# A 16-head attention inside a long kernel: batch 1's projections and splits moved in front of the loop

## The reference

```
Q, K, V = x @ Wq.T + bq, x @ Wk.T + bk, x @ Wv.T + bv      # split into 16 heads of 16
lam = 10 * exp(-5 * u_prev);  use_sparse = lam >= 1
dense  = softmax(Q K^T / 4 + lam * (mask ? 0 : -1)) V
sparse = softmax over 32 chosen keys per query (with their multiplicity) V
out = where(use_sparse, sparse, dense) @ Wo.T + bo
```

## Time and profile before

| | us |
|---|---|
| median of 3 runs (2247.75 to 2248.11) | 2247.83 |
| the profiled execution | 2237.77 |
| its span | 2235.9 |
| TensorE busy | 1931.1 (86%) |
| VectorE busy | 1138.5 (51%) |
| ScalarE busy | 933.5 (42%) |
| POOL busy | 441.0 (20%) |

### The profile page before, as it was taken

One profiled execution on the slowest core, in us unless ns is written; L12 is line 12 of the kernel. 1 busy time (PEld: TensorE's weight loads), 2 busy tenths in 40 slices (PEclk: granted clock), 3 DMA queues, 4 the chain that ended last, 5 costly groups with the idle time before them and its releaser, 6 DMA issues.

```text
span 2235.9 us, 37687 instructions
## 1 busy us (share of the span) xinstructions
PE 1931.1 (86%) x15745; PEld 1387.0 (62%) x15745; DVE 1138.5 (51%) x2327; ACT 933.5 (42%) x1618; POOL 441.0 (20%) x490
## 2 busy tenths in 40 slices
PE   3889978978988835988999999969999999999956
PEld 2357874664655613656776767747777777777734
DVE  3474532034322144777887888825455433545342
ACT  1303012102322113756887888824444433444221
POOL 1342100004210052111121221102222221222112
PEclk9879568988999966999999999989999999999978
DMA  4000021202333337111034011020000000000001
GB/s 120 0 1 1 1 62 39 79 19 75 113 105 93 99 115 113 34 46 46 23 58 57 24 35 31 5 83 1 1 1 1 1 1 1 1 1 1 16 9 38
DMA packets 84906, 86.95 MB, mean 39 GB/s; under 512 B 34370, under 2 KB 70658, under 8 KB 84610
## 3 DMA queue, kind: packets, MB, share of 16 engines
q1 hardware_dynamic: 81666, 76.16, 13.1%
q0 software_dynamic: 3072, 8.39, 1.3%
HBM read 65.65 MB, written 18.87 MB: 38 GB/s over the span
## 4 chain that ended last, share of the span: by engine, by line
PE 70%; DVE 18%; issue 5%; DMA 4%; ACT 2%; POOL 1%; SPq 1%; DVEq 0%; POOLq 0%; ACTq 0%
PE PS L1037 7%; PE PS L1029 6%; DVE arena L1675 6%; PE PS L1862 6%; PE PS L1846 6%; PE PS L1521 5%; PE PS L1811 5%; PE PS L1836 5%; PE PS L1534 5%; DVE arena L1680 3%; PE PS L524 3%; PE PS L1513 3%; PE PS L1870 3%; PE PS L1816 3%; PE PS L477 1%
## 5 line engine op out<-in xcount | busy, mean ns | idle before, releaser
L1675 DVE CUSTOM_DVE_ANT_0 arena<-PS,arena 128x1024 f32<-128x1024 f32 x256 | 312.6, 1221 | 79.6 <-PE PS L1513 70.1
L1521 PE MATMUL PS<-arena 128*128 128x128 f32 x2048 | 283.7, 277 | 35.2 <-DVE arena L1680 34.9
L1521 PEld LDWEIGHTS PS<-arena 128*128 128x128 f32 x2048 | 242.4, 143 | 102.9 <-DVE arena L1680 45.9
L1608 ACT ACTIVATE arena<-arena 128x1024 f32<-128x1024 f32 x256 | 295.0, 1152 | 25.3 <-DVE arena L1675 25.1
L1928 ACT ACTIVATE arena<-arena 128x449 f32<-128x449 f32 (+1 forms) x256 | 162.5, 635 | 213.0 <-DVE arena L1960 213.0
L2011 POOL TENSOR_SCALAR arena<-arena 128x448 f32<-128x448 f32 (+1 forms) x256 | 153.6, 612 | 450.4 <-DVE arena L1951 450.4
L1960 DVE CUSTOM_DVE_ANT_0 arena<-PS,arena 128x448 f32<-128x448 f32 (+1 forms) x256 | 141.2, 590 | 148.6 <-PE PS L1837 148.6
L1604 ACT COPY arena<-PS 128x512 f32<-128x512 f32 x256 | 150.4, 588 | 118.4 <-PE PS L1521 111.5
L1680 DVE COPY arena<-PS 128x512 f32<-128x512 f32 x256 | 175.8, 687 | 1.2 <-PE PS L1521 1.2
L1029 PE MATMUL PS<-arena 128*128 128x512 f32 x384 | 170.1, 601 | 6.6 <-ACT arena L1128 6.6
L1513 PE MATMUL PS<-arena 96*128 96x512 bf16 x512 | 157.1, 389 | 18.6 <-issue 18.0
(11 more groups left out here) (255 smaller groups left out, 2681.9 us busy)
## 6 DMA issues: line engine op xcount, KB each, us to landing
arena<-in_L_ffn_W SPq DMA_DIRECT2D x16, 1024.0 KB, 6.3
arena<-prior SPq DMA_DIRECT2D x16, 512.0 KB, 4.2
parts<-arena SPq DMA_DIRECT2D x12, 512.0 KB, 4.3
arena<-parts SPq DMA_DIRECT2D x48, 128.0 KB, 5.4
arena<-parts SPq DMA_DIRECT2D x96, 64.0 KB, 3.1
ye<-arena SPq DMA_DIRECT2D x8, 512.0 KB, 3.5
prior<-arena SPq DMA_DIRECT2D x4, 1024.0 KB, 9.0
arena<-in_xT SPq DMA_DIRECT2D x2, 1024.0 KB, 9.6
```

What stands on the lines that cost most here:

```text
L1521: h = e.transpose(PS[:, i, P * j:P * j + P], Sb[z % 3][:, 512 * g + P * j:512 * g + P * j + P], ident)
L1608: e.activation(Sb[z % 3], Sb[z % 3], ACT.Exp, bias=mr[:, z % 4:z % 4 + 1], scale=-1.0).then_inc(s_exp, 1)
L1675: e.tensor_tensor_reduce(Sb[z % 3], ps, Ab[m % 2], 1.0, 3e38, ALU.add, ALU.min, mr[:, z % 4:z % 4 + 1]).then_inc(s_ttr, 1)
```

## The change

- Both batches' preparation stands in front of the loop, as one list `PREP`: for batch 0, four transposes (T), four projection groups of Q, four of K (P), four of V; for batch 1 the same with K ahead of Q. It uses the program's ring of eight banks (`pring = K.ring`). The loop holds no preparation.
- The split goes by pieces of 128x512. ScalarE writes the high part straight from PSUM with the bias (`high`); VectorE makes PSUM + bias - high in one instruction (`rest`), into `R1`; ScalarE casts it to the middle part (`middle`); VectorE subtracts for the low part (`low`). Each engine puts piece n + 1's first step ahead of piece n's second step. `R1`, `HM` and `LO` exist twice, one for even and one for odd projections.
- The factor -0.25 is put into Wq and bq once, by two ScalarE instructions at the start.
- `prepared`: TensorE and VectorE wait until all preparation groups are emptied, before the loop.
- Stores go by halves (c = 0, 1), with a semaphore each. SP's order: weights, bias tile 0, Q's stores, K's first store, Q's loads for tile 0, K's second store, K's loads with u after the first six, Q's loads for tile 1, batch 1's four stores. The loads of batch 1's K go into a second `K6`, and stand in tile 1 without a wait for scores.
- VectorE does batch 1's row additions one tile behind each P step of batch 0. In SBUF, temporary buffers share space with the loop's (`xT4` with `Sb` and `Pt`, `R1` and `HM` with the second `K6`, the weights with `Oc`).

```diff
+    K6 = [arena.up(8 * S).bitcast(BF16).rearrange("p (h s) -> p h s", h=16)]
...
+    k6b = arena.up(8 * S)
+    K6.append(k6b.bitcast(BF16).rearrange("p (h s) -> p h s", h=16))
...
+    QK = [("q", 0), ("k", 0), ("k", 1), ("q", 1)]
+    KO, QO = [1, 2], [0, 3]
+    pring = K.ring
+    def prep_steps():
+        def part(b, os):
+            return [("T", b, j) for j in range(4)] + [("P", o, c, n) for o in os for c, n in CN] + [("V", b, j) for j in range(4)]
+        return part(0, (0, 1)) + part(1, (2, 3))
...
 sp:
+        get_bias(0)
+        for c in range(2):
+            store(0, c)
+        store(1, 0)
+        get_q(0)
+        store(1, 1)
         for g4 in range(4):
             get_k(0, g4)
-        K.combined(w, 1)
-        e.dma_start(ub[:, 0:B], ...)
-        get_bias(0)
-        store(0, 1)
-        get_q(0)
+            if g4 == 0:
+                K.combined(w, 1)
+                e.dma_start(ub[:, 0:B], ...)
         get_q(1)
+        for o in (2, 3):
+            for c in range(2):
+                store(o, c)
         for z in range(NZ):
-            if second(z) in (12, 20):
-                store(1, second(z) // 8 - 1)
...
-            if m == TB_ - 1 and h % 4 == 3:
-                w.wait_ge(s_sc, z + 1)
+            if m == 1 and h % 4 == 1:
+                stored(w, 2)
+                stored(w, 3)
                 get_k(1, h // 4)
...
 pe:
-        for k in range(24):
-            prep(0, k)
-        K.combined(w, 1)
+        for s in PREP:
+            prep(s)
+        prepared(w)
         for z in range(NZ + 15):
-            if second(z) is not None:
-                prep(1, second(z))
...
 act:
+        def high(s):
+            _, o, c, n = s
+            if o >= 2:
+                w.wait_ge(s_fp[o - 2][c], 48)
+            bias = cv("bk", c) if QK[o][0] == "k" else bqs[:, c:c + 1]
+            e.activation(HM[o % 2][:, 0, c, 512 * n:512 * n + 512], PS[:, group(s, pring), :], ACT.Identity, bias=bias).then_inc(s_hi, 1)
+        def middle(s):
+            _, o, c, n = s
+            w.wait_ge(*pring.emptied(s))
+            e.copy(HM[o % 2][:, 1, c, 512 * n:512 * n + 512], R1[o % 2][:, c, 512 * n:512 * n + 512]).then_inc(s_mid, 1)
+        def prep():
...
+            for s in PREP:
+                if s[0] == "T":
+                    e.copy(xT4[s[1]][:, s[2] % 2, 512 * (s[2] // 2):512 * (s[2] // 2) + 512], PS[:, group(s, pring), :]).then_inc(pring.into(s), 1)
+                if s[0] == "P":
+                    high(s)
+                if last:
+                    middle(last)
+                last = s if s[0] == "P" else None
...
 dve:
+        def rest(s):
+            _, o, c, n = s
+            w.wait_ge(s_hi, CHUNK[s] + 1)
+            if o >= 2:
+                w.wait_ge(s_mid, CHUNK[s] - 7)
+            bias = cv("bk", c) if QK[o][0] == "k" else bqs[:, c:c + 1]
+            e.scalar_tensor_tensor(out=R1[o % 2][:, c, 512 * n:512 * n + 512], in0=PS[:, group(s, pring), :], scalar=bias,
+                                   in1=HM[o % 2][:, 0, c, 512 * n:512 * n + 512], op0=ALU.add, op1=ALU.subtract).then_inc(pring.into(s), 1)
+        def low(s):
+            _, o, c, n = s
+            w.wait_ge(s_mid, CHUNK[s] + 1)
+            e.tensor_tensor(LO[o % 2][:, c, 512 * n:512 * n + 512], R1[o % 2][:, c, 512 * n:512 * n + 512], HM[o % 2][:, 1, c, 512 * n:512 * n + 512], ALU.subtract).then_inc(s_lo, 1)
+        def prep():
+            last = None
+            for s in PREP:
+                if s[0] == "P":
+                    rest(s)
+                if last:
+                    low(last)
+                last = s if s[0] == "P" else None
+                if s[0] == "V":
...
+                if s[1] == 0 and s[0] != "T" and added:
+                    K.add_rows(e, w, added.pop(0))
+            prepared(w)
+            e.memset(PS[:, OBK, :], 0.0).then_inc(s_oz, 1)
```

More of the change, by code:

```diff
@@ new lines, in phase_e @@
+    Wo4 = arena.up(2 * D).rearrange("p (c n) -> p c n", c=2)
+    Oc_ = arena.up(2 * S)
+    Oc = Oc_.rearrange("p (t c) -> p t c", t=TB_)
+    loop = arena.up(11 * S)
+    Sb = [loop[:, S * j:S * j + S] for j in range(3)]
+    Pt = [loop[:, S * j:S * j + S] for j in range(3, 11)]
+    k6b = arena.up(8 * S)
+    K6.append(k6b.bitcast(BF16).rearrange("p (h s) -> p h s", h=16))
+    Tb = arena.up(S)
+    OT = arena.up(512)
+    mr, rc, ub = arena.up(8), arena.up(16), arena.up(16)
+    Ab = [arena.up(S) for _ in range(2)]
@@ L1353, in phase_e @@
[L1353 to L1358, removed]
+    Wq4, Wk4, Wv4 = (Oc_[:, 2 * D * j:2 * D * j + 2 * D].rearrange("p (c n) -> p c n", c=2) for j in range(3))
+    bvb = Oc_[:, 6 * D:7 * D]
+    xT4 = [loop[:, 2 * S * j:2 * S * j + 2 * S].rearrange("p (c s) -> p c s", c=2) for j in range(B)]
@@ L1368, in phase_e, with prepared, stored @@
     s_ab = [K.sem(f"e_a{j}") for j in range(2)]
[L1371 to L1382, removed]
+    QK = [("q", 0), ("k", 0), ("k", 1), ("q", 1)]
+    KO, QO = [1, 2], [0, 3]
+    CN = [(c, n) for c in range(2) for n in range(2)]
+    pring = K.ring
[3 more added lines that the diff above has]
+        return part(0, (0, 1)) + part(1, (2, 3))
+    PREP = prep_steps()
+    CHUNK = {s: n for n, s in enumerate(z for z in PREP if z[0] == "P")}
+    for s in PREP:
+        pring.plan(s, "act" if s[0] == "T" else "dve")
+    def prepared(w):
+        for s in PREP[-8:]:
+            w.wait_ge(*pring.emptied(s))
+    def stored(w, o):
+        for c in range(2):
+            w.wait_ge(s_fp[o][c], 48)
     def closing(z):
@@ L1556, in close @@
             h.then_inc(ring.sem, 1)
-        for s, n in K.d_last:
-            w.wait_ge(s, n)
-        for k in range(24):
-            prep(0, k)
-        K.combined(w, 1)
+        for s in PREP:
+            prep(s)
+        prepared(w)
         for z in range(NZ + 15):
-            if second(z) is not None:
-                prep(1, second(z))
             if z < NZ:
@@ L1625, in close @@
                 e.activation(X4T[b][:, c, 512 * n:512 * n + 512], PS[:, i, :], ACT.Identity, bias=cv("bo", c)).then_inc(ring.into(key), 1)
-        for k in range(20):
-            prep(0, k)
-        K.combined(w, 1)
+        prep()
         w.wait_ge(s_u, 16)
@@ L1690, in normal @@
             e.tensor_tensor(Oc[:, m % TB_, :].rearrange("p (h j) -> p h j", h=16), ov[:, :, 0:16], rc.unsqueeze(2).broadcast_to([P, 16, 16]), ALU.mult).then_inc(ring.into(key), 1)
[L1692 to L1698 removed]
+        added = list(range(TB_, 2 * TB_))
+        prep()
         for z in range(NZ + 15):
[L1700 to L1701 removed]
             if z < NZ:
```

147 lines of the change are left out of this document (49 added, 98 removed).

## The result

The changed kernel takes 2187.34 us (median of 4 runs, 2185.13 to 2196.52) against 2247.97 us for the kernel before: ratio 0.973, 95% interval 0.970 to 0.977, or 60.6 us less. Predicted were 2184.6 us and 63.2 us less.

A forecast was written before the change was run, and what follows sets the result against it. TensorE was taken to set the loop's pace, with batch 1's preparation stalling tiles 1 to 4 and waits filling the front. Front 18.7 plus loop 44.5, together 63.2 us, off the 2247.83 us median gave 2184.6; range 2176 to 2206.

The forecast's parts named there:

- The loop, -44.5: Tiles 1 to 4, freed of batch 1's preparation, run at 33.41 us each: 44.5 us less.
- the 24 loads of batch 1's K move from tile 7 to tile 1; in tile 7 they cost nothing that can be seen: In the loop, these loads were given no cost, since the three tiles that give 33.41 us contain them.
- rival (d): Loop stalls come back as waits for batch 1's stores and loads in tiles 0 and 1: 2229.1 us; chance 0.05.
- The front, -18.7: From first transposes, the first addition comes at 855.1 against 873.82, with both batches prepared: 18.7 us less.
- my own mark: The forecast falls if the front ends after 865 or tiles 1 to 4 take more than 140 us.
- now stand one behind each projection piece of batch 0: In the front, eight pairs of row additions on VectorE, 2 x 0.48 us each, the last ending near 826.3.
- The unit prices: Front, per piece of 512: fused subtraction 0.75, last subtraction 0.69, high part 0.69, middle 0.6; projection group 1.72 us.
- u's chain: End of the front: from u's exponential to POOL's bias takes 9.3 us, bias at 855.0, releasing the first addition.
- (a): In the front, a piece's links run in series, 2.9 us each: time 2201.7 us; chance 0.12.
- (b): DMA late again in the front: u still lands at 861.8, first addition 871.2, time 2200.7 us; chance 0.06.
- (c): TensorE at half clock in all of the front, 47.9 us more: time 2230.8 us; chance 0.08, in part or whole.
- (e): Slower: half clock in the front goes on into the loop; over the first whole tile 2262.8 us; chance 0.03.

The follow-up runs named there:

- loop_without_prep: Kernel before with batch 1's preparation left out of the loop (batch 1 works on batch 0's Q, K and V): 2199.91 us, ratio 0.9805.
- adds: Changed kernel with one pair of row additions behind every projection piece of batch 0, instead of behind Q's pieces and V's additions: ratio 0.9724 to the kernel before.
- u_early: Changed kernel with u's DMA ahead of the first bias tile and its exponential ahead of the pieces: ratio 0.9729 to the kernel before.
- serial: Changed kernel with each piece's four links (high, rest, middle, low) issued in a row, without overlapping the next piece: 2191.32 us, ratio 0.9766.
- combine_first: Changed kernel with all row additions ahead of the first transposes: ratio 0.9817 to the kernel before.
- all_three: Changed kernel with batch 1's K loads spread over tiles 1 to 4, row additions behind every batch 0 projection piece, u exponentiated first: ratio 0.9706.

## Why the prediction was right, and where it was not

**The loop, -44.5.** Right by mechanism and size: 134.0 us in `loop_without_prep`, and 33.41 us for tiles 2 to 4 of after. The pace of the undisturbed tiles was the right price. The step that failed is "the 24 loads of batch 1's K move from tile 7 to tile 1; in tile 7 they cost nothing that can be seen". In tile 7 the loads of before stood behind waits for a buffer that came free group by group; with a second buffer nothing paces them, and they cost 5.6 us in tile 1 (39.05). Their issues show it: four groups of six, at 1156.3, 1164.6, 1173.3 and 1181.5, in before, and all 24 from 904.6 to 916.5 in after. It is rival (d) at an eighth of its price, by a mechanism that I did not have.

**The front, -18.7.** It gave 6.9. By my own mark (tiles 1 to 4 under 140 us, the front's end by 865) the loop holds and the front fails: 872.2, or 866.9 with the 5.3 us of earlier stages taken off. From the first transposes on, predicted and measured: V of batch 0 ends at 25.5 and 33.6 (the hole and the half clock behind it +9.4, V -1.2 us), batch 1's transposes start at 25.5 and 36.1 (the row additions +2.4), u's exponential at 43.7 and 55.6 (the half clock of 844 to 848 +1.1), the first addition at 53.2 and 65.0.

- The hole had no row in the trace of before, where the copies came at once. It is the largest part of what was missed.
- The row additions: "now stand one behind each projection piece of batch 0" is wrong, as is the same statement in the description of the change. The condition `s[1] == 0` holds for the four pieces of Q and then for the four steps of V, so the last pair came at 35.9, not 24.4 (of which some 9 is the hole). `adds` shows what that costs: 4.2 us.
- The unit prices held. The new fused subtraction, bounded by 0.75 and 0.96:

```profile
L1662 DVE SCALAR_TENSOR_TENSOR arena<-PS,arena x16: 741/750/752, 819.8 to 861.4; 128x512 f32<-128x512 f32 x16
```

ScalarE's high part took 0.69, its middle one 0.61 (taken: 0.6), VectorE's low part 0.68 (taken: 0.69). That the low part costs more than half of its 1.22 us at double width is the fixed cost per instruction of "VectorE: DVE Perf Modes", section "The TRN2 errata", of the Trainium skill; the trace agrees, by 0.07 us a half.
- u's chain took 872.18 - 862.79 = 9.4 us (predicted 9.3) and set the end, as predicted; `u_early` shows 2.7 us behind it.

**The rivals.** (a) Did not happen, and `serial` shows that it costs 7 us, not the 17.1 between 2184.6 and 2201.7. (b) Did not happen: u lay ready for 12.7 us. (c) Happened in two places: after the hole (the projections of 819.34 start at 0.85 us a record and reach 0.43 near 824), and over 844 to 848. In both TensorE had stood idle before. "TensorE: Matmul & The Clock Gate", section "What's actually happening", of the Trainium skill has throttled as the default that activity lifts; the trace agrees (0.57 in 844 to 848, behind 2.43 us of idle, and 0.99 in 848 to 872, with TensorE at work). (e) Did not happen: the clock was at 0.53 in 872 to 879, as at the loop's start in before, then at 1.00, except for the 3.4 us behind the stop in tile 1; the window 943 to 1143 has 1.00.

**The sum.** 63.2 us predicted, 60.6 measured between medians, 45.8 in the two stages of the profiled executions. For the profiled execution the prediction's sum gave 2174.6 us; it took 2196.5. That the median came out near is luck: the stages gave 17.5 us less than the sum has, and some 14 us of difference between the medians that no stage of the change shows made up for it. The range, 2176 to 2206, held both medians of after, 2184.4 and 2187.3.

## What to carry to other kernels

Where some turns of a loop hold extra work and others don't, the pace of the plain turns prices the removal: it came within 1 us of 44.5 here. A second buffer removes a wait and with it the pacing of the loads that stood behind it, so put the loads where they come in small groups, and look through a tile of the loop for a stop without a releaser. Read a condition in the diff with each value it can take before pricing where its instructions stand, and compare profiled executions from an event that both share, since what lies before it wanders (here the first transposes started between 795.8 and 807.9 us, `combine_first` aside, though the stages ahead of the attention are the same).

## What the runs showed of the hardware that I had not expected

- Behind 24 loads issued within 12 us TensorE stood still in the middle of a group of matmuls, with no semaphore to wait for, in eight of nine profiles, for 2.00 to 3.63 us. In the changed kernel the 16 KB packets of the instruction queue came 18.6 and 12.6 us apart there, later in the loop 8 to 13, and in all eight TensorE went on 1.3 to 1.9 us after such a packet had ended. With six loads at a time it never stood still.
- The release of two ScalarE copies by TensorE's transposes came late in nine profiles: 5.7 to 11.4 us after the transposes had started in eight, 9 and 19 us in `loop_without_prep`; in five, that of before among them, they came within 4 us. The profile puts the waits down to "issue", "remote" or TensorE. A start at half clock and gathers of POOL stood beside it in all nine, but also in before and in `all_three`, where it is absent. Open.
- `ACT_TABLE_LOAD` takes 1.28 us, and the exponential behind it starts at once (862.79 + 1.29 = 864.08).
